# Row maxima turned in a bank of their own, and the first expert tile's up products moved ahead of the last attention outputs

## The chip, the cores and the metric

The kernel runs on one core of a Trainium2 chip. The metric is the device time of one execution in microseconds (us): three runs of the kernel before gave 564.69, 566.49 and 567.13 us, median 566.49 us. The engines are named as the profile names them: PE (TensorE, matrix products), PEld (its weight loads), DVE (VectorE), ACT (ScalarE), POOL (GpSimd) and SP (SyncE, which here only issues transfers). They run side by side, each through its own list of instructions in order, and wait for one another at counters (semaphores).

## The reference

Sixteen sequences of 256 tokens of width 128 go through a mixture-of-experts layer, causal attention with 16 heads of width 8, and the same mixture-of-experts layer again:

```python
x = L0_attn_x                                   # (16, 256, 128)
x = x + 0.5 * _L0_ffn_ref(_layernorm(x), gate_w, w1, w2, w3)   # 8 experts, the best 2 of each token
x = x + _L0_attn_ref(_layernorm(x), WQ, WK, WV, WO)
x = x + 0.5 * _L0_ffn_ref(_layernorm(x), gate_w, w1, w2, w3)

# attention: score = QK^T / sqrt(8) + causal mask; score -= rowmax(score); softmax; times V; times WO
# experts:   y = (silu(x w1) * (x w3)) w2 for each expert, weighted by the two gates
```

## The kernel before

The program has three stages. In the first (to about 183 us of the profiled execution) the tokens are routed and go through the experts in tiles of 256 rows, called units; the second (about 183 to 409 us) is attention; the third is the second expert layer, again in units. One unit is `tile_up`, 12 matmuls into the banks `B_H1` and `B_H3`, then a SiLU on ACT, a product on DVE, and `tile_down`. A tile's rows come from memory through a transposing load that SP issues (`load`, L476); SP issues the first load of the third stage only when the last scores are done and every scattered row of that set has landed (L526).

Attention runs as 16 steps, `step(b, ...)` with b from 0 to 15, one for each sequence. A step has eight rounds (u on PE, k on DVE), one for each pair of heads. In a round PE makes a pair's scores for a sequence that is up to two steps ahead (`score_products`, L1753, with `score_masks`, L1770); DVE takes their row maxima (`row_max`, L1322), and there is a single buffer for these scores, so that the next pair's scores wait for this reduction. PE also makes the transposed scores of sequence b itself (`score_t_products`, L1783, and L1790 and L1792 for the mask), ACT takes their exponentials (L953), and PE multiplies these by the values (`values`, L1816 and L1819).

Two chains run beside this and share PSUM bank 7, `B_M1`, whose uses are counted by `m1_ready` (written) and `m1_freed` (read):

- The row maxima of sequence b+1: in round 3 DVE combines them (`combine_max`, L1330 to L1332), POOL clamps them (`clamp`, L698), in round 4 PE turns them (`max_transpose`, L1801 to L1803), ACT copies them out (L941), and SP places them for the next step's products.
- The outputs of sequence b-1: in rounds 1 and 3 PE turns their halves back (`o_back`, L1831), each is normalised by DVE (`o_norm`, L1339 and L1341), in round 5 PE turns both (`o_transpose`, L1838), ACT and DVE copy them out as a high and a low half (L945, L1347), in round 7 PE multiplies by WO (`o_project`), and DVE adds to x (`x_add`, L1351).

So bank 7 has five uses in a step: half 0, half 1, the maxima, the transposed outputs, the projection. A use waits until the use before has been freed, and `max_transpose` waits for two things, the clamp and the second `o_norm`:

```python
            def max_transpose(b, q, use):
                pe.wait_ge(clamp_done, done(b))
                if not isinstance(use, int) or use > 0:
                    pe.wait_ge(m1_freed, use)
```

In the steps without a previous sequence or without a next one, `no_use` counts an empty use on DVE, ACT and PE.

Behind step 15 the last outputs are finished between the first units of the third stage. PE's order there is written out by hand: `values(15, 3, 3)`, both `o_back`, `tile_up(2, 0)`, `o_transpose`, `tile_up(2, 1)`, `o_project`, `tile_up(2, 2)`, and then `tile_down` and `tile_up` in turn. DVE's order beside it is `highest` (gates of a routed set), `o_norm` of half 0, `second` (more gates, L1142 to L1149), `o_norm` of half 1, `product` of unit 0. The units' banks 0 to 3 are the banks of the scores and transposed scores; bank 4, free in attention, takes every second `tile_down` of the units.

Of the kernel before, what the change touches and what calls it, by code (L numbers as in the profile page):

```python
# [38 lines left out]
SEQ = 256  # L39
# [7 lines left out]
PAIRS = 8  # L47
# [58 lines left out]
def build_macaron(nc, x_in, w_up1, w_up3, w_down, w_small, out, batches):  # L106
# [8 lines left out]
    with ctx:  # L115
# [188 lines left out]
        m1_ready = sem("m1_ready")  # L304
        m1_freed = sem("m1_freed")
# [128 lines left out]
        def m1_use(b):  # L434
            return 5 * b - 1

        def max_use(b):

            return m1_use(b) + 2
# [3 lines left out]
        def max_bank(use):  # L443

            return B_M1 if use else B_EARLY
# [3 lines left out]
        def _(sp):  # L449
# [311 lines left out]
        def _(act):  # L761
# [174 lines left out]
            def max_copy(b, q, use):  # L936

                act.wait_ge(m1_ready, done(use))
                if not isinstance(b, int) or b > 1:
                    act.wait_ge(m_placed, 32 * (b - 1))  # L940
                s_.activation(negmax_t[0:HEADS, q % 2, :], bank[0:HEADS, max_bank(use), 0:SEQ], ACT.Copy).then_inc(m1_freed, 1)  # L941
# [5 lines left out]
            def step(b, q, G, prev=True, route=None):  # L947
                for u in range(PAIRS):
# [17 lines left out]
                    if u == 4:  # L966
                        if b_ok(b + 1):
                            max_copy(b + 1, q + 1, max_use(b))
                        else:
                            no_use(act, max_use(b), m1_freed)  # L970
                        if route is not None:
                            rows_high(1, route)
                    if u == 5:
                        if prev:
                            o_high(m1_use(b) + 3)
                        o_copy(b, q, 0)
# [5 lines left out]
            def first_groups(n):  # L982
                g, which = first_step(n)
                if which == 0:
                    x_high(m0_use(g), g)
                if which == 1:
                    q_high(g, g)
                if which == 2:
                    k_high(g, g)
                if which == 3:  # L990
                    act.wait_ge(vaug_set, 2)
                    v_copy(g, g)
                if n == MAX_TURN + 1:
                    max_copy(0, 0, 0)
# [47 lines left out]
        def _(dve):  # L1042
# [306 lines left out]
            def x_add(b, u0, tail=False):  # L1349
                dve.wait_ge(m1_ready, done(u0 + (3 if tail else 4)))  # L1350
                v_.scalar_tensor_tensor(x_tile(tile_of(b - 1), 2), bank[:, B_M1, 0:2 * D], 1.0 / WSCALE,  # L1351
                                        x_tile(tile_of(b - 1), 2), ALU.mult, ALU.add).then_inc(m1_freed, 1)

            def step(b, q, G, prev=True, adds=(), route=None, buf=None):
                odd = q % 2 == 1
                for k in range(PAIRS):
# [18 lines left out]
                    if not prev and k == 7:  # L1375
                        no_use(dve, max_use(b) + 1, m1_freed)
                        no_use(dve, max_use(b) + 2, m1_freed)
                    if k in (5, 7) and adds:
                        add(*adds[k // 7])
                    if route is not None:  # L1380
                        if k == 0:

                            dve.wait_ge(m1_freed, m1_use(b - 1) + 5)
                            statistics(1, route, buf)
# [87 lines left out]
            x_add(batches, M1_TAIL, tail=True)  # L1472
# [34 lines left out]
        def _(pe):  # L1507
# [288 lines left out]
            def max_transpose(b, q, use):  # L1796
                pe.wait_ge(clamp_done, done(b))
                if not isinstance(use, int) or use > 0:
                    pe.wait_ge(m1_freed, use)
                dst = bank[0:HEADS, max_bank(use), 0:SEQ]  # L1800
# [3 lines left out]
                    .then_inc(m1_ready, 1)  # L1804
# [20 lines left out]
            def o_back(b, q, u0, qb):  # L1825
# [3 lines left out]
                pe.wait_ge(m1_freed, use)  # L1829
# [18 lines left out]
            def step(b, q, G, prev=True, route=None):  # L1848
                par = (q // 2 + 1) % 2
                for u in range(PAIRS):  # L1850
# [16 lines left out]
                    if u == 4:  # L1867
                        if b_ok(b + 1):
                            max_transpose(b + 1, q + 1, max_use(b))
                        else:  # L1870
# [10 lines left out]
                    if u == 7:  # L1881
                        if route is not None:
                            gate(route)
                        if prev:
                            o_project(m1_use(b) + 4)
                        else:
                            for use in (max_use(b) + 1, max_use(b) + 2):
                                pe.wait_ge(m1_freed, use)
                                no_use(pe, use, m1_ready)
# [7 lines left out]
            def first_groups(n):  # L1897
# [13 lines left out]
                if n == MAX_TURN:  # L1911
                    pe.wait_ge(s_reduced, done(PAIRS + AHEAD - 1, D_S))
                    max_transpose(0, 0, 0)
# [63 lines left out]
```

## Time and profile before

| | |
|---|---|
| median of 3 runs | 566.49 us (564.69 to 567.13) |
| the profiled execution's own time | 565.05 us |
| its span in the trace | 563.0 us |
| PE busy | 501.2 us, 89% of the span |
| DVE, ACT, POOL busy | 373.7, 317.2, 267.9 us |
| granted TensorE clock, mean | 0.993 of full speed |

The span is the stretch that the trace covers; 2.05 us of the execution's time lie outside it. A time given as "at 409.6" is counted from the start of the span. The busy shares are means over stages that have different limits, so what an edit is worth is read in its own stage.

### The profile page before, as it was taken

The numbers are of one execution on the slowest core, as the hardware profiler recorded it, in microseconds if no ns is written. First come the engines' busy times: TensorE is split into PE (matmuls) and PEld (weight loads), VectorE is DVE, ScalarE is ACT, GpSimd is POOL, SyncE is SP. The second block draws the span as 40 slices with busy tenths as digits, with TensorE's granted clock in tenths as the row PEclk, the third lists the DMA queues.
The fourth block names the chain that finished last, engine by engine and source line by source line (L and its number), as shares of the span: only waits on it lengthen the run. The fifth ranks groups of instructions, "written<-read, shape, count | busy, mean of one in ns | idle before, by whom it ended". The sixth has DMA issues, their size and how long they took to land.

```text
span 563.0 us, 19023 instructions
## 1 busy us (share of the span) xinstructions
PE 501.2 (89%) x7286; PEld 411.0 (73%) x7286; DVE 373.7 (66%) x995; ACT 317.2 (56%) x597; POOL 267.9 (48%) x325
## 2 busy tenths in 40 slices
PE   1689999999999788898889886888889999999995
PEld 1679998988889456565656554655579999999995
DVE  5656865324675789999898898776375532455665
ACT  4945654433335576767676765667744444445553
POOL 7967877612463323333431111565607601666662
PEclk9999999999999799999999999999999999999999
DMA  9971247786764314846212120311147755843222
GB/s 271 306 242 50 61 100 161 175 157 155 129 138 121 102 59 108 245 109 186 79 58 62 41 60 2 119 57 36 45 94 164 155 133 130 156 119 91 72 75 56
DMA packets 114661, 65.86 MB, mean 117 GB/s; under 512 B 51856, under 2 KB 108432, under 8 KB 114576
## 3 DMA queue, kind: packets, MB, share of 16 engines
q1 hardware_dynamic: 84400, 38.95, 27.0%
q0 software_dynamic: 6912, 14.17, 10.0%
q10 hardware_dynamic: 23264, 11.54, 8.3%
q8 instruction: 61, 1.00, 0.8%
q14 instruction: 24, 0.20, 0.1%
HBM read 18.88 MB, written 34.87 MB: 95 GB/s over the span
## 4 chain that ended last, share of the span: by engine, by line
PE 61%; DVE 20%; ACT 6%; DMA 5%; issue 4%; POOL 1%; SPq 1%; ACTq 0%; DVEq 0%; POOLq 0%
PE bank L1641 19%; PE bank L1522 10%; PE bank L1524 10%; PE bank L1523 10%; DVE negmax L1322 8%; ACT pt L953 3%; PE bank L1753 3%; PE bank L1534 2%; PE bank L1816 2%; PE bank L1783 2%; DMA yg<-sorted_y,row 2%; DVE X L1219 2%; PE bank L1831 1%; ACT r_xn L785 1%; ACT ot L933 1%
## 5 line engine op out<-in xcount | busy, mean ns | idle before, releaser
L689 POOL DMA_INDIRECT yg<-sorted_y,row x108 | 104.1, 964 | 141.7 <-PE bank L1641 45.7
L1210 DVE SCALAR_TENSOR_TENSOR pt<-bank,pt 128x512 f32<-128x512 f32 x122 | 84.3, 691 | 118.3 <-PE bank L1524 109.8
L953 ACT ACTIVATE pt<-bank 128x768 f32<-128x768 f32 x128 | 104.1, 813 | 72.2 <-PE bank L1792 71.7
L675 POOL DMA_INDIRECT sorted_x<-xs,row x108 | 106.5, 987 | 52.0 <-issue 22.5
L1641 PE MATMUL bank<-w,pt 128*128 (+1 forms) x976 | 130.0, 277 | 0.0
L1641 PEld LDWEIGHTS bank<-w,pt 128*128 128x128 f32 x976 | 118.6, 192 | 3.2
L1322 DVE TENSOR_REDUCE negmax<-bank 128x10 f32<-128x640 f32 x128 | 104.4, 816 | 17.1 <-PE bank L1770 15.3
L829 ACT ACTIVATE pt<-bank 128x512 f32<-128x512 f32 x122 | 72.8, 597 | 26.3 <-PE bank L1524 25.1
L837 ACT ACTIVATE yb<-bank 128x256 f32<-128x256 f32 x82 | 31.5, 384 | 79.5 <-PE bank L1641 72.9
L1753 PE MATMUL bank<-zc 63*64 63x64 f16 (+3 forms) x1024 | 43.0, 244 | 16.6 <-DVE negmax L1322 13.8
L1753 PEld LDWEIGHTS bank<-zc 63*64 63x64 f16 x1024 | 18.9, 105 | 43.6 <-DVE negmax L1322 29.3
L1783 PE MATMUL bank<-zc 64*64 64x256 f16 (+1 forms) x1024 | 44.1, 248 | 3.5 <-ACT pt L953 3.2
L1816 PE MATMUL bank<-pt,vaug 128*32 128x256 f32 x512 | 41.5, 394 | 5.1 <-ACT ot L933 4.8
L1522 PE MATMUL bank<-pt,w1h 128*128 128x256 f16 x164 | 45.0, 274 | 1.0 <-DMA pt<-sorted_x 0.7
L1523 PE MATMUL bank<-pt,w3h 128*128 128x256 f16 x164 | 45.0, 275 | 0.0
L1524 PE MATMUL bank<-pt,w1l 128*128 128x256 f16 x164 | 45.0, 275 | 0.0
L1522 PE MATMUL bank<-pt,w3h 128*128 128x256 f16 x164 | 45.0, 275 | 0.0
L1523 PE MATMUL bank<-pt,w1h 128*128 128x256 f16 x164 | 45.0, 274 | 0.0
L1524 PE MATMUL bank<-pt,w3l 128*128 128x256 f16 x164 | 45.0, 274 | 0.0
L858 ACT ACTIVATE ot<-bank,comb 128x128 f32<-128x128 f32 x80 | 25.1, 364 | 35.1 <-PE bank L1641 35.1
L1219 DVE SCALAR_TENSOR_TENSOR X<-yg,weight,X 128x128 f32<-128x128 f32 x108 | 37.7, 349 | 3.4 <-DMA yg<-sorted_y,row 1.4
L1792 PE MATMUL bank<-causal_t,ident_b 64*64 64x256 bf16 x256 | 35.8, 273 | 0.0
(171 smaller groups left out, 1015.8 us busy)
## 6 DMA issues: line engine op xcount, KB each, us to landing
sorted_y<-yb ACTq DMA_DIRECT2D x82, 128.0 KB
sorted_x<-zeros SPq DMA_DIRECT2D x2, 2944.0 KB, 14.5
zc<-qk_rows SPq DMA_DIRECT2D x84, 64.0 KB
qk_rows<-qksplit SPq DMA_DIRECT2D x8, 512.0 KB, 2.8
sorted_x<-zeros SPq DMA_DIRECT2D x1, 2432.0 KB, 11.4
sorted_x<-zeros SPq DMA_DIRECT2D x1, 2176.0 KB, 10.3
X<-x_in SPq DMA_DIRECT2D x8, 256.0 KB, 5.1
zc<-w_up SPq DMA_DIRECT2D x8, 256.0 KB, 6.7
```

Of the source, the lines that this page charges most:

```text
L675: ps.indirect_dma_start(out=sorted_x[s], out_offset=bass.IndirectOffsetOnAxis(ap=row[:, s, k, t:t + 1], axis=0), in_=xs[:, R0[s] + t, :], ...
L689: ps.indirect_dma_start(out=yg[:, a % D_YG, k, :], out_offset=None, in_=sorted_y[s], in_offset=bass.IndirectOffsetOnAxis(ap=row[:, s, k, t ...
L829: s_.activation(silu[:, n % D_H], bank[:, B_H1 + n % 2, :], ACT.Silu, scale=1.0 / WSCALE)\
L953: s_.activation(pt[:, hg, (u % 2) * 768:(u % 2 + 1) * 768].rearrange("p (a n) -> p a n", a=2), bank[:, B_ST:B_ST + 2, 0:384], ACT.Exp, sca ...
L1210: v_.scalar_tensor_tensor(hid[:, n % D_HID], bank[:, B_H3 + n % 2, :], 1.0 / WSCALE, silu[:, n % D_H], ALU.mult, ALU.mult).then_inc(prod_d ...
L1322: v_.tensor_reduce(negmax[:, q % 2, k, :, 0:PARTS], bank[:, b0:b0 + 2, 0:S_COLS].rearrange("p a (s k) -> p a s k", k=HALF), AX.X, ALU.max, ...
L1522: t_.matmul(dst, ah, bh, start=True, stop=False)
L1523: t_.matmul(dst, ah, bl, start=False, stop=False)
L1524: return t_.matmul(dst, al, bh, start=False, stop=True)
L1641: last = t_.matmul(y_half(n)[:, u * D:(u + 1) * D], hid[:, n % D_HID, c * SLOTS + u * P:c * SLOTS + (u + 1) * P], w2[:, bass.ds(offset + c ...
L1753: t_.matmul(bank[side(g), b0 + a, c0:c0 + keys], zc[rows, par, 0, u, q0:q0 + HALF], zc[rows, par, 1, u, e * SEQ:e * SEQ + keys], start=n = ...
L1783: t_.matmul(bank[side(g), B_ST + a, kb * SEQ:SEQ + kb * P], zc[side(a), par, 1, u, k0 + HALF * g:k0 + HALF * (g + 1)], zc[side(a), par, 0, ...
```

## The change

The turned maxima move from bank 7 to bank 4 and get counters of their own, `max_ready` and `max_freed`; bank 7 keeps four uses in a step, and `no_use` goes. In the hand-written order behind step 15, `tile_up(2, 0)` and its wait move ahead of both `o_back`. DVE's, ACT's, POOL's and SP's own orders stay as they were.

```diff
-        def no_use(eng, use, count):
-            if count is m1_freed:
-                eng.wait_ge(m1_freed, use)
-                eng.wait_ge(m1_ready, use + 1)
-            eng.sem_inc(count, 1)
...
         def m1_use(b):
-            return 5 * b - 1
-        def max_use(b):
-            return m1_use(b) + 2
+            return 4 * b - 4
...
-        def max_bank(use):
-            return B_M1 if use else B_EARLY
+        B_MAX = 4
+
+        def max_bank(b):
+            return B_MAX if b else B_EARLY
...
-                hold(sp, m1_freed, (max_use(b - 1) + 1) if not isinstance(b, int) or b > 0 else 1)
+                hold(sp, max_freed, b + 1)
...
-            def max_copy(b, q, use):
-                act.wait_ge(m1_ready, done(use))
+            def max_copy(b, q):
+                act.wait_ge(max_ready, b + 1)
...
-            def max_transpose(b, q, use):
+            def max_transpose(b, q):
                 pe.wait_ge(clamp_done, done(b))
-                if not isinstance(use, int) or use > 0:
-                    pe.wait_ge(m1_freed, use)
-                dst = bank[0:HEADS, max_bank(use), 0:SEQ]
+                if b > 1:
+                    pe.wait_ge(max_freed, b)
+                dst = bank[0:HEADS, max_bank(b), 0:SEQ]
...
-                            max_transpose(b + 1, q + 1, max_use(b))
-                        else:
-                            pe.wait_ge(m1_freed, max_use(b))
-                            no_use(pe, max_use(b), m1_ready)
+                            max_transpose(b + 1, q + 1)
                     if u == 5 and prev:
-                        o_transpose(m1_use(b) + 3)
+                        o_transpose(m1_use(b) + 2)
...
             values(batches - 1, 3, 3)
+            pe.wait_ge(exp_done, done(PAIRS * batches - 1, D_ST))
+            tile_up(2, 0)
             o_back(batches, 0, M1_TAIL, 0)
             o_back(batches, 0, M1_TAIL, 1)
-            pe.wait_ge(exp_done, done(PAIRS * batches - 1, D_ST))
-            tile_up(2, 0)
             o_transpose(M1_TAIL + 2)
             tile_up(2, 1)
```

The order of PE's instructions in round 4 of step 2, of the kernel before: the last masks of the transposed scores, the three products that turn the maxima, and the first of `values`.

```order
L1790 MATMUL bank<-causal_t,ident_b 64x2x64
L1792 MATMUL bank<-causal_t,ident_b 64x2x128
L1801 MATMUL bank<-ident_h,negmax_h 16x128 [waits m1_freed,clamp_done]
L1802 MATMUL bank<-ident_h,negmax_h 16x64
L1803 MATMUL bank<-ident_h,negmax_h 16x64
L1816 MATMUL bank<-pt,vaug 32x256 [waits exp_done]
```

And of the changed kernel, whose line numbers are 11 lower here:

```order
L1779 MATMUL bank<-causal_t,ident_b 64x2x64
L1781 MATMUL bank<-causal_t,ident_b 64x2x128
L1790 MATMUL bank<-ident_h,negmax_h 16x128 [waits max_freed,clamp_done]
L1791 MATMUL bank<-ident_h,negmax_h 16x64
L1792 MATMUL bank<-ident_h,negmax_h 16x64
L1805 MATMUL bank<-pt,vaug 32x256 [waits exp_done]
```

No instruction moved; the first product waits for `max_freed` in place of `m1_freed`, and for the clamp as before.

PE's order behind step 15, of the kernel before: the end of `values`, both `o_back` (L1831), and the first products of `tile_up(2, 0)`, which start with a wait for the first load (`xt_loaded6`).

```order
L1819 MATMUL bank<-pt,vaug 32x128 x4
L1831 MATMUL bank<-ident,ot 128x128 [waits m1_freed,o_copied]
L1831 MATMUL bank<-ident,ot 128x128 x3
L1831 MATMUL bank<-ident,ot 128x128 [waits m1_freed,o_copied]
L1831 MATMUL bank<-ident,ot 128x128 x3
L1522 ISA [waits silu_done,xt_loaded6,exp_done]
L1522 MATMUL bank<-qksplit,w1h 128x256
L1523 MATMUL bank<-qksplit,w1h 128x256
```

The changed kernel at the same place:

```order
L1808 MATMUL bank<-pt,vaug 32x128 x4
L1511 ISA [waits silu_done,xt_loaded6,exp_done]
L1511 MATMUL bank<-qksplit,w1h 128x256
L1512 MATMUL bank<-qksplit,w1h 128x256
```

The wait for the load now stands ahead of both `o_back`.

Further on in the changed kernel, from the last products of `tile_up(2, 0)` to the wait at the head of `tile_up(2, 1)`:

```order
L1513 REGISTER_ALU
L1513 MATMUL bank<-qksplit,w3l 128x256
L1821 MATMUL bank<-ident,ot 128x128 [waits m1_freed,o_copied]
L1821 MATMUL bank<-ident,ot 128x128 x3
L1821 MATMUL bank<-ident,ot 128x128 [waits m1_freed,o_copied]
L1821 MATMUL bank<-ident,ot 128x128 x3
L1828 MATMUL bank<-ident,on 128x128 [waits m1_freed]
L1828 MATMUL bank<-ident,on 128x128
L1511 ISA [waits silu_done,xt_loaded7]
```

Both `o_back` (L1821) and `o_transpose` (L1828) now follow one another with no unit's products between them.

## Rows read from the trace of the kernel before

**Rows 1.** The page's head, busy times and chain that ended last, whole execution.

```profile
span 563.0 us, 19023 instructions
PE 501.2 (89%) x7286; PEld 411.0 (73%) x7286; DVE 373.7 (66%) x995; ACT 317.2 (56%) x597; POOL 267.9 (48%) x325
...
PE 61%; DVE 20%; ACT 6%; DMA 5%; issue 4%; POOL 1%; SPq 1%; ACTq 0%; DVEq 0%; POOLq 0%
```

**Rows 2.** Busy time by stretch: attention, then experts; length first, then each engine.

```profile
183.00:403.00 220.00, 186.25 (x4385) 124.39 (x4387) 185.83 (x501) 144.20 (x225) 82.22 (x102) 0.98 0.30 86
...
420.00:553.00 133.00, 133.00 (x1214) 124.82 (x1214) 69.34 (x162) 65.30 (x145) 68.98 (x72) 1.00 0.52 120
```

**Rows 3.** Who waited for whom, 180 to 440: total us, times, longest.

```profile
PE bank L1753 <- DVE negmax L1322: 13.8, 33, 1.4
...
PE bank L1801 <- DVE on L1341: 5.4, 13, 0.6
```

**Rows 4.** Timeline of step 4, round 4: start, duration, instruction, idle before and releaser.

```profile
247.81 0.29 DVE L1341 TENSOR_TENSOR on<-bank,rden 128x128 f32<-128x128 f32 x1
...
247.63 0.35 POOL L698 TENSOR_SCALAR negmax_h<-negmax 128x32 f16<-128x32 f32 x1 [1.25 <-DVE negmax L1332]
...
248.24 0.22 PE L1801 MATMUL bank<-ident_h,negmax_h 128*16 128x128 f16 x1 [0.17 <-DVE on L1341]
...
249.10 0.33 PE L1753 MATMUL bank<-zc 63*64 63x64 f16 x8
```

**Rows 5.** The same of step 3, round 4.

```profile
233.89 0.29 DVE L1341 TENSOR_TENSOR on<-bank,rden 128x128 f32<-128x128 f32 x1
...
233.76 0.35 POOL L698 TENSOR_SCALAR negmax_h<-negmax 128x32 f16<-128x32 f32 x1 [2.54 <-DVE negmax L1332]
...
234.32 0.22 PE L1801 MATMUL bank<-ident_h,negmax_h 128*16 128x128 f16 x1 [0.64 <-DVE on L1341]
...
235.51 0.33 PE L1753 MATMUL bank<-zc 63*64 63x64 f16 x8 [0.26 <-DVE negmax L1322]
```

**Rows 6.** PE's timeline behind step 15.

```profile
409.19 0.40 PE L1819 MATMUL bank<-pt,vaug 128*32 128x128 f32 x8
410.31 0.66 PE L1831 MATMUL bank<-ident,ot 128*128 128x128 f32 x4 [0.72 <-ACT ot L933]
411.80 0.63 PE L1831 MATMUL bank<-ident,ot 128*128 128x128 f32 x4 [0.84 <-DVE on L1341]
412.26 0.27 PE L1522 MATMUL bank<-qksplit,w1h 128*128 128x256 f16 x1
...
414.08 0.44 PE L1838 MATMUL bank<-ident,on 128*128 128x128 f32 x2 [0.34 <-DVE on L1341]
414.35 0.27 PE L1522 MATMUL bank<-qksplit,w1h 128*128 128x256 f16 x1
...
415.66 0.22 PE L1522 MATMUL bank<-wsh,oh 128*128 128x128 f16 x1
```

**Rows 7.** DVE's timeline beside it.

```profile
411.07 0.26 DVE L1339 RECIPROCAL rden<-bank 128x16 f32<-128x16 f32 x1 [0.56 <-PE bank L1831]
411.37 0.29 DVE L1341 TENSOR_TENSOR on<-bank,rden 128x128 f32<-128x128 f32 x1
...
413.73 0.29 DVE L1341 TENSOR_TENSOR on<-bank,rden 128x128 f32<-128x128 f32 x1
413.94 0.68 DVE L1210 SCALAR_TENSOR_TENSOR pt<-bank,pt 128x512 f32<-128x512 f32 x1
```

**Rows 8.** SP's first loads of the third stage, L476, 408 to 426.

```profile
L476 SPq DMA_TRANSPOSE qksplit<-sorted_x x12: 1215/1264/1981, 408.5 to 424.5; - x12
...
DMA to landing us min/median/max: 2.7/2.7/4.6
```

**Rows 9.** Around step 0: busy time, granted clock third from the end; PE's timeline.

```profile
186.00:192.80 6.80, 6.13 (x96) 3.81 (x100) 4.37 (x16) 2.85 (x5) 3.33 (x5) 0.50 0.43 112
192.80:196.00 3.20, 2.07 (x68) 1.36 (x60) 2.79 (x8) 2.71 (x5) 2.22 (x3) 1.00 0.11 28
...
183.77 0.33 PE L1753 MATMUL bank<-zc 63*64 63x64 f16 x8 [0.53 <-issue]
...
185.08 0.33 PE L1753 MATMUL bank<-zc 63*64 63x64 f16 x8 [0.65 <-DVE negmax L1322]
...
186.34 0.54 PE L1783 MATMUL bank<-zc 64*64 64x256 f16 x8 [0.87 <-ACT pt L953]
```

More of the change, by code:

```diff
@@ L304, in build_macaron @@
         m1_ready = sem("m1_ready")
+        max_ready = sem("max_ready")
+        max_freed = sem("max_freed")
         m1_freed = sem("m1_freed")
@@ L934, in o_copy @@
                              bank[:, B_O, :], ACT.Copy).then_inc(o_copied, 1)
-            def max_copy(b, q, use):
-                act.wait_ge(m1_ready, done(use))
+            def max_copy(b, q):
+                act.wait_ge(max_ready, b + 1)
                 if not isinstance(b, int) or b > 1:
                     act.wait_ge(m_placed, 32 * (b - 1))
-                s_.activation(negmax_t[0:HEADS, q % 2, :], bank[0:HEADS, max_bank(use), 0:SEQ], ACT.Copy).then_inc(m1_freed, 1)
+                s_.activation(negmax_t[0:HEADS, q % 2, :], bank[0:HEADS, max_bank(b), 0:SEQ], ACT.Copy)\
+                    .then_inc(max_freed, 1)
             def o_high(use):
@@ L974, in step @@
                         if prev:
-                            o_high(m1_use(b) + 3)
+                            o_high(m1_use(b) + 2)
                         o_copy(b, q, 0)
@@ L993, in first_groups @@
                 if n == MAX_TURN + 1:
-                    max_copy(0, 0, 0)
+                    max_copy(0, 0)
             def first_stack(n):
@@ L1347, in o_low, with x_add @@
                 v_.tensor_tensor(ol[:, :], bank[:, B_M1, 0:SEQ], oh[:, :], ALU.subtract).then_inc(m1_freed, 1)
-            def x_add(b, u0, tail=False):
-                dve.wait_ge(m1_ready, done(u0 + (3 if tail else 4)))
+            def x_add(b, u0):
+                dve.wait_ge(m1_ready, done(u0 + 3))
                 v_.scalar_tensor_tensor(x_tile(tile_of(b - 1), 2), bank[:, B_M1, 0:2 * D], 1.0 / WSCALE,
@@ L1374, in step @@
                         add(0, EARLY + k // 2)
-                    if not prev and k == 7:
-                        no_use(dve, max_use(b) + 1, m1_freed)
-                        no_use(dve, max_use(b) + 2, m1_freed)
                     if k in (5, 7) and adds:
@@ L1381, in step @@
                         if k == 0:
-                            dve.wait_ge(m1_freed, m1_use(b - 1) + 5)
+                            dve.wait_ge(m1_freed, m1_use(b - 1) + 4)
                             statistics(1, route, buf)
@@ L1471, in _ @@
             product(U_SECOND + 1)
-            x_add(batches, M1_TAIL, tail=True)
+            x_add(batches, M1_TAIL)
             product(U_SECOND + 2)
@@ L1803, in max_transpose @@
                 t_.matmul(dst[:, P + HALF:SEQ], negmax_h[:, q % 2, 1, :], ident_h[:, 0:HALF], start=True, stop=True)\
-                    .then_inc(m1_ready, 1)
+                    .then_inc(max_ready, 1)
             def values(b, q, hg):
@@ L1828, in o_back @@
                 pe.wait_ge(o_copied, done(2 * (b - 1) + 1, D_O))
-                pe.wait_ge(m1_freed, use)
+                if use > 0:
+                    pe.wait_ge(m1_freed, use)
                 for hg in range(HG):
@@ L1884, in step @@
                         if prev:
[L1885 to L1889, printed above, removed]
+                            o_project(m1_use(b) + 3)
                     if b == ROUTED + 2:
@@ L1912, in first_groups @@
                     pe.wait_ge(s_reduced, done(PAIRS + AHEAD - 1, D_S))
-                    max_transpose(0, 0, 0)
+                    max_transpose(0, 0)
             def first_set(slot):
```

4 lines of the change are left out of this document (1 added, 3 removed).

## The prediction

> **What bounds the kernel now.** I read the page's head first: PE is busy for 501.2 of 563.0 us and carries 61% of the chain that ended last [rows 1]. Then the stretches. From 420 to 553 PE is busy for all of the 133.00 us, at full clock: the second expert layer is PE's own work without a gap, so whatever delays PE's entry into it comes out in the end time one for one, and nothing behind gives it back. In attention neither engine is full: from 183 to 403 PE is busy for 186.25 and DVE for 185.83 of 220 us [rows 2]. They take turns, since PE's next scores wait for DVE's reduction of the last (33 waits, 13.8 us in all) [rows 3]. So a gap on PE that closes in attention counts only where PE, and not DVE, ends last in the round behind it.
>
> The list of waits then shows what the first part of the change touches: PE sat idle 5.4 us in 13 waits before L1801, the turning of the maxima, put down to L1341, the second normalisation [rows 3]. The timeline of PE, DVE and SP behind step 15 is the last view, because the second part reorders PE there.
>
> **Part 1: the maxima leave bank 7.** The removed wait is the one for L1341. What remains is the clamp on POOL. In step 4 the clamp ends at 247.63 + 0.35 = 247.98 and the normalisation at 247.81 + 0.29 = 248.10; PE starts the turning at 248.24, 0.14 after the later of them [rows 4]. In step 3 the clamp ends at 234.11, the normalisation at 234.18, and PE starts at 234.32 [rows 5]. So the wait that takes the place of the removed one ends 0.12 and 0.07 us earlier, not 0.4. These two steps are one of each kind, odd and even, and both engines run the same two lists of instructions in all 14 steps that have the turning and a previous sequence, so I take 0.1 us a step and not more.
>
> Does the 0.1 reach the end? In step 4 PE goes from the turning through the value products into the next scores at 249.10 without a wait, so PE is last there and 0.1 us is won [rows 4]. In step 3 the next scores start at 235.51 after 0.26 us of idling for DVE's reduction, which doesn't depend on the turning; there nothing is won [rows 5]. With half of the 14 steps like step 4 that is 7 x 0.1 = 0.7 us at most; some of it is lost again at later waits for DVE, and I take 0.5. The bounds are 0 (every such 0.1 us ends in a wait for DVE) and 14 x 0.12 = 1.7 us (none does).
>
> Other edits of this part cost nothing. The turned outputs in round 5 waited for ACT's copy of the maxima and now wait for the second normalisation, an earlier event, and PE has no idle row there. The copy, the placing and their transfers follow the turning by the same instructions. The empty uses of steps 0 and 15 carried no work. Bank 4 is not written by a unit in attention.
>
> The Trainium skill speaks for this part (Perfetto Trace Analysis, Optimizing Tensor Performance, Matmuls): independent groups of matmuls should rotate through different PSUM banks, so that one bank's evacuation overlaps the next group's products. By that rule the whole listed wait would go. The trace doesn't agree, as the two clamp rows show: with the bank free, the data is not there yet.
>
> **Part 2: `tile_up(2, 0)` ahead of both `o_back`.** Before, PE ends `values` at 409.59, waits 0.72 us for ACT's copy, runs the first `o_back` from 410.31, waits 0.84 us for the first normalisation, runs the second from 411.80 and goes straight into `tile_up(2, 0)` at 412.26. That fills the time in which DVE works through `second`: the second normalisation ends only at 413.73 + 0.29 = 414.02, `o_transpose` starts at 414.08 after 0.34 us, and PE is dense from there [rows 6, 7].
>
> The idea to fill the 0.72 us with unit 0 meets the load. SP issues the first one at 408.5, and such loads land 2.7 us after issue in the median here, also at the least [rows 8]: 408.47 + 2.7 = 411.2. PE runs its list in order, so both `o_back` now stand behind a wait that ends at 411.2 instead of 410.3. Step by step:
>
> - `tile_up(2, 0)` starts at 411.2. Its 12 matmuls take as long as those of `tile_up(2, 1)`, from 414.35 to the next product at 415.66: 1.31 us [rows 6]. So the first `o_back` starts at 412.5.
> - From the start of the first `o_back` to DVE's reciprocal are 411.07 - 410.31 = 0.76 us, and from there to the end of the second normalisation 414.02 - 411.07 = 2.95, since `second` stands between the two on DVE [rows 6, 7]. That gives 412.5 + 0.76 + 2.95 = 416.2. The second `o_back` (at 411.80 - 411.07 = 0.73 behind the reciprocal, so 414.0) is long done.
> - `o_transpose` starts 0.06 later, at 416.3, against 414.08: 2.2 us later. In between PE idles from about 414.6 to 416.3, where `tile_up(2, 0)` used to be.
>
> Behind `o_transpose` both orders are equal, the product of unit 0 (413.94 before) moves with the second normalisation and is still in time for unit 2, and PE is the bound. So the handover costs 2.2 us. Its bounds: if the load had landed before 409.6, PE would go into it at once, the first `o_back` would start at 410.9 in place of 410.31, and the cost would be 0.6; if it landed 4.6 us after issue, the longest such time [rows 8], 1.9 us more, 4.1. I stay with 2.2, as the two loads in flight are those of before and nothing new runs beside them.
>
> **Sum.** Against the profiled execution, 565.05 us (563.0 of span and 2.05 around it): -0.5 + 2.2 = +1.7, so 566.8. That execution was 1.4 us under the median of the runs; on the median the forecast is 566.5 + 1.7 = 568.2 us, 0.3% more. What a measurement of this kernel can tell from no change is about 0.5%, or 2.8 us.
>
> **The rivals.**
> *The clock falls in the handover (slower).* Around step 0 PE idled 0.53, 0.65 and 0.87 us between short bursts, 2.05 us out of some 3.1, and from 186.0 to 192.8 the granted clock was 0.50, 1.2 GHz [rows 9]. In my schedule PE idles 0.8 and 1.7 us between 413.2 and 416.3, 2.5 out of 3.1; so the stretch is at least as empty, while the one of before, with 0.72, 0.84 and 0.34 [rows 6], kept 2.4 GHz. What follows is dense work on the bound engine, where a stretch at half clock loses half of itself: 3.4 us for one as long as 6.8, 1.7 for one half as long. That gives 569.9 to 571.6 us. Against it: the expert products between the gaps are denser than what ran in step 0. [...] Chance 0.28. The Trainium skill (Perfetto Trace Analysis, Matmul Optimizations) says that this engine scales with its utilization, so that matmuls should run back to back in batches; the rows of step 0 agree.
> *The bank was the wait (faster).* All 5.4 us before L1801 vanish: 566.5 + 2.2 - 5.4 = 563.3. For it speaks the list of waits, against it the end of the clamp in both steps. Chance 0.04.
> *The load is hidden (no change).* If it lands about 1 us sooner than the median says, the handover costs 0.6 and the steps give 0.5: 566.6. Nothing in the rows has one landing under 2.7. Chance 0.10.
> *The load is late.* 4.6 us: 568.2 + 1.9 = 570.1. Chance 0.05.
>
> **How the numbers follow.** My forecast has 0.50; 0.03 is left for what I don't see. The time is that of the forecast, 568.2. The range runs from 566.3, just under the hidden load (566.6) and the forecast with the full 1.7 us from the steps (567.0), to 571.0, inside the clock's case, whose shorter stretch is the likelier one. Faster by over 0.5% (under 563.7): 0.04. Slower by over 0.5% (over 569.3): the clock's case but for a little, part of the late load, and the forecast's upper edge, 0.29. Within: 0.67.
>
> **What would show each step.** In the changed profile the wait before the turning (now L1790) is put down to POOL's clamp, with 4 to 5 us in 13 or 14 waits; if it is under 2 us, the bank was the wait. Attention, from its first scores to the end of the last `values`, is 0 to 1.7 us shorter. Behind step 15 PE waits for the load, for some 1.6 us from the end of `values`, the first products of unit 0 come 0.9 us after the place where the first `o_back` stood, `o_transpose` waits some 1.7 us for L1341's successor, and comes 6.7 us behind the end of `values` where it was 4.5. The granted clock of the following 7 us is 1.00, or 0.50 in part if the rival holds. The prediction is wrong if PE doesn't wait for the load, if the second expert layer has gaps that take the delay in, or if the steps change by more than 2 us either way.

## The result and the profile after

The changed kernel takes 569.42 us (median of 6 runs, 568.0 to 570.29). The kernel before, run beside it on the same chip, takes 565.62 us (6 runs, 562.46 to 567.13). The ratio is 1.0074, with a 95% interval of 1.0047 to 1.0101: the change makes the kernel 3.8 us slower, where 1.7 were forecast. (A ratio here and below is worked out from the runs and is not the quotient of the two medians, which is 1.0067; a difference in us is one of medians.) The profiled execution took 569.17 us against 565.05, 4.1 more, so its trace holds the whole loss.

The page's head of the changed kernel, to be laid beside [rows 1], and its two stretches beside [rows 2]:

```profile
span 567.1 us, 19015 instructions
PE 505.5 (89%) x7286; PEld 412.6 (73%) x7286; DVE 373.8 (66%) x995; ACT 316.3 (56%) x597; POOL 267.9 (47%) x325
```

```profile
183.00:403.00 220.00, 188.88 (x4404) 125.40 (x4406) 186.11 (x501) 144.24 (x226) 82.26 (x102) 0.99 0.31 89
420.00:553.00 133.00, 133.00 (x1225) 124.91 (x1223) 69.80 (x168) 64.77 (x144) 66.69 (x71) 1.00 0.51 119
```

The second expert layer is as full as before, 133.00 of 133.00 us at full clock, so nothing behind the handover gave anything back. The loss lies ahead of that stretch. PE's timeline behind step 15, beside [rows 6], shows where:

```profile
409.20 0.40 PE L1808 MATMUL bank<-pt,vaug 128*32 128x128 f32 x8
411.56 0.28 PE L1511 MATMUL bank<-qksplit,w1h 128*128 128x256 f16 x1 [1.96 <-issue]
...
412.88 0.60 PE L1821 MATMUL bank<-ident,ot 128*128 128x128 f32 x4
414.31 0.63 PE L1821 MATMUL bank<-ident,ot 128*128 128x128 f32 x4 [0.83 <-DVE on L1333]
416.58 0.69 PE L1828 MATMUL bank<-ident,on 128*128 128x128 f32 x2 [1.64 <-DVE on L1333]
417.06 0.42 PE L1511 MATMUL bank<-qksplit,w1h 128*128 128x256 f16 x1
```

PE ends `values` at 409.60, the same time as before, waits 1.96 us for the first load, and makes `tile_up(2, 0)` and both `o_back`; `o_transpose` starts at 416.58 against 414.08. The profile puts the 1.96 us down to "issue"; that it is the wait for the load follows from the order of the instructions and from the load's issue at 408.66, 2.9 us before these products. In the seven traces in which PE waits at this place, the products start 2.8 to 3.0 us behind the issue. The last two rows show a second thing: `o_transpose` takes 0.69 us where it took 0.44, and a product of a unit 0.42 where it took 0.27. PE works slower there. The windows behind it say the same, with the granted clock third from the end (0.51, the 1.2 GHz level, then 0.99, the 2.4 GHz level):

```profile
416.40:419.80 3.40, 3.22 (x16) 2.41 (x17) 1.15 (x3) 0.98 (x2) 0.00 (x0) 0.51 0.36 82
419.80:424.00 4.20, 4.20 (x51) 3.92 (x49) 2.99 (x12) 1.68 (x4) 0.30 (x2) 0.99 0.29 62
```

DVE's timeline beside it answers to [rows 7]. The second normalisation (L1333) stands behind the gates, as it did, and so follows the first by 2.4 us wherever that starts:

```profile
413.58 0.26 DVE L1331 RECIPROCAL rden<-bank 128x16 f32<-128x16 f32 x1 [3.07 <-PE bank L1821]
413.88 0.29 DVE L1333 TENSOR_TENSOR on<-bank,rden 128x128 f32<-128x128 f32 x1
...
416.24 0.29 DVE L1333 TENSOR_TENSOR on<-bank,rden 128x128 f32<-128x128 f32 x1
```

The last long block of products of PE's stage closes the account. It is L1641 before and L1630 after; the first row is of before, the second of after:

```profile
554.11 2.94 PE L1641 MATMUL bank<-w,pt 128*128 128x128 f32 x24
```

```profile
558.19 2.93 PE L1630 MATMUL bank<-w,pt 128*128 128x128 f32 x24
```

From the end of `values` to this block are 554.11 - 409.59 = 144.5 us before and 558.19 - 409.60 = 148.6 after, 4.1 more. Of these, 2.5 lie ahead of `o_transpose` (6.98 us behind the end of `values`, against 4.49), and 1.6 behind it (141.61 to the block, against 140.03). The second part fits the stretch at half clock: 3.4 us long, and half of it lost.

In attention the first part of the change can be read off the waits and the timeline. The list of waits before the turning, beside [rows 3], 195 to 403 us:

```profile
PE bank L1742 <- DVE negmax L1314: 13.8, 30, 1.4
...
PE bank L1790 <- POOL negmax_h L691: 5.3, 9, 1.8
```

Then the two steps of [rows 4] and [rows 5], step 4 first, then step 3, and the turning and the next scores of step 5, since the row of those scores is missing in step 3. The third fence is step 5 of the kernel before:

```profile
249.10 0.35 POOL L691 TENSOR_SCALAR negmax_h<-negmax 128x32 f16<-128x32 f32 x1 [1.25 <-DVE negmax L1324]
249.28 0.29 DVE L1333 TENSOR_TENSOR on<-bank,rden 128x128 f32<-128x128 f32 x1
249.51 0.22 PE L1790 MATMUL bank<-ident_h,negmax_h 128*16 128x128 f16 x1
```

```profile
234.18 0.35 POOL L691 TENSOR_SCALAR negmax_h<-negmax 128x32 f16<-128x32 f32 x1 [2.52 <-DVE negmax L1324]
234.59 0.22 PE L1790 MATMUL bank<-ident_h,negmax_h 128*16 128x128 f16 x1 [0.48 <-POOL negmax_h L691]
...
263.35 0.22 PE L1790 MATMUL bank<-ident_h,negmax_h 128*16 128x128 f16 x1 [0.48 <-POOL negmax_h L691]
264.70 0.33 PE L1742 MATMUL bank<-zc 63*64 63x64 f16 x8 [0.41 <-DVE negmax L1314]
```

```profile
262.03 0.22 PE L1801 MATMUL bank<-ident_h,negmax_h 128*16 128x128 f16 x1 [0.41 <-DVE on L1341]
...
263.22 0.33 PE L1753 MATMUL bank<-zc 63*64 63x64 f16 x8 [0.27 <-DVE negmax L1322]
```

The bank is free, and the clamp sets the start. In step 4 it ends at 249.45, PE starts at 249.51, before the normalisation is over (249.57), and no idle time is left where 0.17 us stood. In step 3 the idle time falls from 0.64 to 0.48. In step 5 the next scores wait 0.41 for DVE where they waited 0.27: what the turning won, the next wait takes.

### The profile page after: what moved, and what is told of

Same layout as the page of the kernel before. It is cut to its first block, busy times and chain, and to the rows that moved or that the text cites. A ratio compares the mean times of both kernels' runs of the same rounds, so it can differ in the third digit from the quotient of the medians.

```text
span 567.1 us, 19015 instructions
## 1 busy us (share of the span) xinstructions
PE 505.5 (89%) x7286; PEld 412.6 (73%) x7286; DVE 373.8 (66%) x995; ACT 316.3 (56%) x597; POOL 267.9 (47%) x325
## 4 chain that ended last, share of the span: by engine, by line
PE 62%; DVE 21%; ACT 5%; issue 5%; DMA 4%; POOL 1%; SPq 1%; ACTq 0%; DVEq 0%; POOLq 0%
PE bank L1630 18%; PE bank L1511 10%; PE bank L1513 10%; PE bank L1512 10%; DVE negmax L1314 8%; PE bank L1742 3%; ACT pt L947 2%; PE bank L1523 2%; PE bank L1805 2%; DVE X L1211 2%; PE bank L1772 1%; PE bank L1821 1%; ACT r_xn L778 1%; DVE xn L1058 1%; DVE rden L1331 1%
## 5 line engine op out<-in xcount | busy, mean ns | idle before, releaser
L1630 PE MATMUL bank<-w,pt 128*128 (+1 forms) x976 | 130.0, 277 | 0.0
L1630 PEld LDWEIGHTS bank<-w,pt 128*128 128x128 f32 x976 | 118.6, 192 | 3.1
```

Source lines behind the costliest of these rows:

```text
L1630: last = t_.matmul(y_half(n)[:, u * D:(u + 1) * D], hid[:, n % D_HID, c * SLOTS + u * P:c * SLOTS + (u + 1) * P], w2[:, bass.ds(offset + c ...
```

## The experiments

Each kernel is compared with the kernel before, run in turn with it on the same chip. The first batch and the third met the same conditions (kernel before at 564.59 and 563.98 us); the second ran on another chip, on which the kernel before takes 608.36 us, so its numbers are compared within the batch alone. Each trace is of one execution. Line numbers are those of the changed kernel, but for `order_only`, which has those of before, and `clamp_twice`, whose turning is L1794 and clamp L695.

Two theories stood at the start. **The handover and the clock:** the first expert unit ahead of `o_back` puts a wait for the load, 2.5 us, on PE's path, and the gaps it makes bring the clock down for 1.6 more; the bank costs nothing. **The bank:** the turning, at another time or in another bank, costs something in attention, and part of the loss is there.

### Each part alone

`bank_only` has bank 4 and its counts, with the order behind step 15 as before:

```diff
             values(batches - 1, 3, 3)
-            pe.wait_ge(exp_done, done(PAIRS * batches - 1, D_ST))
-            tile_up(2, 0)
             o_back(batches, 0, M1_TAIL, 0)
             o_back(batches, 0, M1_TAIL, 1)
+            pe.wait_ge(exp_done, done(PAIRS * batches - 1, D_ST))
+            tile_up(2, 0)
             o_transpose(M1_TAIL + 2)
```

> The maxima in bank 4 with their own counts, as in the changed kernel; the order behind step 15 as before. Theory A (the handover and the clock behind it cost, the bank gains a little): 564.6 us against 565.6 before, 0 to 1.7 us faster; the turning starts 0.05 us behind the clamp in place of 0.21 to 0.26, the attention steps from the first turning to the end of the last values are about 1 us shorter, and from there to the transposed outputs it takes 4.5 us as before, at full clock. Theory B (the steps themselves got slower, by a new wait for POOL or a changed balance of PE and DVE, and the handover is only part of it): 566.5 us or more.

Measured: 564.86 us, ratio 1.0008 (0.9981 to 1.0035). `order_only` is the reverse, the kernel before with `tile_up(2, 0)` and its wait ahead of both `o_back`, bank 7 shared as before:

> The up products of the first unit ahead of both turned outputs, the maxima in bank 7 as before. Theory A: the handover is 2.5 us longer (7.0 in place of 4.5 from the end of the last values to the transposed outputs) and the clock falls behind it in most executions, 1.6 us more; 569.5 us, 3 to 4.5 us over before. Theory B: at most 2.5 us over before, 568.1, the rest of the measured loss being the bank's.

Measured: 569.53 us, ratio 1.0079 (1.0050 to 1.0108). The loss is all in the order. The 11 runs lie between 566.4 and 572.4 us, and the only trace is of one at 569.85; whether the clock fell in the quicker ones too is not shown. The trace of `order_only` repeats the handover, gap by gap, and the half clock behind it:

```profile
412.19 0.28 PE L1522 MATMUL bank<-qksplit,w1h 128*128 128x256 f16 x1 [1.80 <-issue]
413.51 0.60 PE L1831 MATMUL bank<-ident,ot 128*128 128x128 f32 x4
414.94 0.63 PE L1831 MATMUL bank<-ident,ot 128*128 128x128 f32 x4 [0.84 <-DVE on L1341]
417.21 0.44 PE L1838 MATMUL bank<-ident,on 128*128 128x128 f32 x2 [1.64 <-DVE on L1341]
```

```profile
417.90:421.20 3.30, 3.30 (x21) 2.51 (x20) 1.49 (x3) 0.77 (x2) 0.00 (x0) 0.50 0.21 48
```

`bank_only` at the same place, behind an `o_transpose` that starts 4.56 us behind the end of `values`, stays at the 2.4 GHz level, and reaches the last block in 144.6 us, as the kernel before:

```profile
412.00:416.00 4.00, 3.76 (x37) 3.50 (x38) 2.53 (x6) 1.58 (x3) 0.00 (x0) 1.00 0.45 103
```

### The gaps filled

`filled` is the changed kernel with products that nobody reads (identity by a tile of `xh`, into bank 4) in the two long gaps. They move no wait. If only the late `o_transpose` costs, the time is that of the change; if the gaps bring the clock down, 1.6 us come back.

```diff
+            def filler(n):
+                for k in range(n):
+                    t_.matmul(bank[:, 4, 0:SEQ], ident_h[:, :], xh[:, 0, 0:SEQ], start=True, stop=True,
+                              skip_group_check=True)
             values(batches - 1, 3, 3)
+            filler(16)
             pe.wait_ge(exp_done, done(PAIRS * batches - 1, D_ST))
             tile_up(2, 0)
             o_back(batches, 0, M1_TAIL, 0)
             o_back(batches, 0, M1_TAIL, 1)
+            filler(14)
             o_transpose(M1_TAIL + 2)
```

> The changed kernel with 16 spare matmuls of 256 columns ahead of the wait for the first load and 14 ahead of the transposed outputs, into bank 4, which nobody reads before it is written anew; they run only where PE idled. If the clock is a part of the loss: granted clock 1.00 behind step 15, 567.3 us, about 1.6 us under the changed kernel, with the transposed outputs still 7.0 us behind the last values. If the gaps cost only their own length: 569.4 as the changed kernel.

Measured: 566.77 us, ratio 1.0039 (1.0018 to 1.0061). Its timeline has both fillers, and `o_transpose` where it was in the changed kernel, 6.89 us behind the end of `values`:

```profile
409.74 1.92 PE L1912 MATMUL bank<-xh,ident_h 128*128 128x256 f16 x16
411.67 0.28 PE L1511 MATMUL bank<-qksplit,w1h 128*128 128x256 f16 x1
...
414.89 1.69 PE L1912 MATMUL bank<-xh,ident_h 128*128 128x256 f16 x14
416.70 0.44 PE L1828 MATMUL bank<-ident,on 128*128 128x128 f32 x2
```

```profile
416.40:419.80 3.40, 3.28 (x33) 2.85 (x32) 2.29 (x5) 1.30 (x3) 0.00 (x0) 1.00 0.36 83
```

The window that stood at 0.51 is at 1.00. The first unit's products start 2.8 us behind the load's issue at 408.86, so the first filler doesn't hold them up. From `o_transpose` to the last block are 556.73 - 416.70 = 140.03 us, the number of the kernel before to the hundredth. So 1.6 us of the loss are the clock's, and the gaps are its cause. The medians agree: 2.2 us over the kernel before beside it, where the changed kernel was 3.8 over. Which of the two gaps it takes is not separated, since `filled` fills both. The Trainium skill (Perfetto Trace Analysis, Matmul Optimizations) says that the matmul engine scales its power with its use and wants products back to back in batches; the two windows agree, 0.51 with the gaps and 1.00 with them filled.

### The second normalisation earlier

`norm_first` is the changed kernel with the second `o_norm` ahead of the gates on DVE, to take the 1.6 us gap away and leave the wait for the load.

```diff
             o_norm(batches, M1_TAIL, 0)
-            second(R0[3], RT[3], 3)
             o_norm(batches, M1_TAIL, 1)
+            second(R0[3], RT[3], 3)
```

> The changed kernel with the second normalisation of the last outputs ahead of the second half of the gates on DVE. If the transposed outputs are late because DVE does the gates between the two normalisations: they come 6.1 us behind the last values in place of 7.0, and the product of unit 0 about 1.4 us later, which unit 2 just meets; with the gap shortened to 0.7 us the clock holds in most executions; 567.2 us. If the load alone sets the handover: 569.4, no change.

Measured: 569.41 us, ratio 1.0073 (1.0049 to 1.0098), a miss. In its trace (567.02 us, one of the quick runs) the gap is 0.68 us, `o_transpose` starts 6.06 us behind the end of `values`, and the clock holds, as expected. But a new wait stands behind it, the third row:

```profile
413.50 0.63 PE L1821 MATMUL bank<-ident,ot 128*128 128x128 f32 x4 [0.84 <-DVE on L1333]
414.80 0.44 PE L1828 MATMUL bank<-ident,on 128*128 128x128 f32 x2 [0.68 <-DVE on L1333]
...
417.62 0.23 PE L1511 MATMUL bank<-wsh,oh 128*128 128x128 f16 x1 [1.06 <-DVE ol L1339]
```

`o_project` waits for DVE's low half, ahead of which the gates and the first unit's product now stand: the delay moved by one wait. The 12 runs lie apart, 5 at 565.85 to 567.58 and 7 at 569.37 to 571.30, and the only trace is of the first five. Whether the clock fell in the seven is not shown: the granted clock is on record only as each run's mean, 0.988 to 0.998 in the five and 0.983 to 0.991 in the seven, which leans that way and doesn't say where it fell. This kernel tells of the moved wait and of nothing else.

### On the second chip

`after_again` is the changed kernel once more.

> The changed kernel once more, beside the next three on one chip, and a second trace of it. 569 us, 3.8 us over before; the transposed outputs 7.0 us behind the last values, and 142.96 us from them to PE's last product if the clock holds there, 144.5 if it falls for 3.4 us. Theory A (order and clock) expects the fall in most executions, so here too.

Measured: 610.92 us, ratio 1.0030 (0.9999 to 1.0061), a smaller loss. In its trace the first load is issued 2.0 us before the end of `values` (in the changed kernel's first trace 0.9), PE waits for it 0.85 us, and `o_transpose` comes 5.9 us behind the end. The half clock is there all the same:

```profile
443.24 0.40 PE L1808 MATMUL bank<-pt,vaug 128*32 128x128 f32 x8
444.49 0.28 PE L1511 MATMUL bank<-qksplit,w1h 128*128 128x256 f16 x1 [0.85 <-issue]
...
449.52 0.44 PE L1828 MATMUL bank<-ident,on 128*128 128x128 f32 x2 [1.65 <-DVE on L1333]
```

```profile
450.20:453.50 3.30, 3.30 (x21) 2.50 (x20) 1.49 (x3) 0.78 (x2) 0.00 (x0) 0.50 0.22 48
```

PE's wait is 1.1 us shorter and `o_transpose` comes 1.1 us sooner than in the first trace, so the handover costs less where the load is issued earlier. That this makes the whole smaller loss is argued: no trace of the kernel before was taken on this chip, and the interval reaches from no loss into that of the first measurement.

`spread` keeps bank 4 and puts each piece where its data is ready: half 0 before the load, unit 0 while DVE normalises, half 1, unit 1 in the time of the gates, then `o_transpose`.

```diff
             values(batches - 1, 3, 3)
+            o_back(batches, 0, M1_TAIL, 0)
             pe.wait_ge(exp_done, done(PAIRS * batches - 1, D_ST))
             tile_up(2, 0)
-            o_back(batches, 0, M1_TAIL, 0)
             o_back(batches, 0, M1_TAIL, 1)
-            o_transpose(M1_TAIL + 2)
             tile_up(2, 1)
-            o_project(M1_TAIL + 3)
+            o_transpose(M1_TAIL + 2)
             tile_up(2, 2)
+            o_project(M1_TAIL + 3)
```

> The maxima in bank 4, and behind step 15 another order: first turned half, up products of unit 0, second turned half, up products of unit 1, transposed outputs, up products of unit 2, projection. If the loss comes from a load's wait ahead of the first turned half and from an empty PE beside DVE's gates, this order has neither: PE idles about 1 us in place of 1.9 behind step 15, clock 1.00, 0.9 us under the kernel with the bank alone and 1 to 2 us under before: 563.2. If any up products ahead of the outputs cost: 565 or more.

Measured: 606.43 us, ratio 0.9968 (0.9937 to 0.9999). In its trace PE has no wait between the first `o_back` and `o_transpose`, and the clock stays at 1.00. `turn_late` has bank 4 and the old order behind step 15, and in round 4 of a step the turning goes behind the value products:

```diff
-                    if u == 4:
-                        if b_ok(b + 1):
-                            max_transpose(b + 1, q + 1)
...
                     if u in (2, 4, 6):
                         values(b, q, u // 2 - 1)
+                    if u == 4:
+                        if b_ok(b + 1):
+                            max_transpose(b + 1, q + 1)
```

> The maxima in bank 4, the order behind step 15 as before, and in each step the turning behind round 4's value products, so that these fill PE's wait for the clamp (0.36 to 0.49 us in every second step). If such a wait pays only where PE ends last: the wait goes, PE's idling before the next scores grows from 0.4 to 0.8 us, and the time stays within 1 us of the kernel with the bank alone, 564.9. If every wait of PE in a step pays: 4 us less, 561.

Measured: 606.47 us, ratio 0.9955 (0.9925 to 0.9986). The wait before the turning is gone, and the next scores wait 0.95 us, where they wait 0.42 in the same step of `spread`:

```profile
283.10 0.22 PE L1790 MATMUL bank<-ident_h,negmax_h 128*16 128x128 f16 x1
284.33 0.33 PE L1742 MATMUL bank<-zc 63*64 63x64 f16 x8 [0.95 <-DVE negmax L1314]
```

`clamp_twice` has bank 4 and the old order too, and POOL does the clamp twice, one behind the other, to see what a later clamp costs.

```diff
                 ps.tensor_scalar(negmax_h[:, q % 2], part[:, 0:PARTS + 1:PARTS, :],
+                                 -MLIMIT, MLIMIT, ALU.max, ALU.min).then_inc(first_clamp, 1)
+                pool.wait_ge(first_clamp, b + 1)
+                ps.tensor_scalar(negmax_h[:, q % 2], part[:, 0:PARTS + 1:PARTS, :],
                                  -MLIMIT, MLIMIT, ALU.max, ALU.min).then_inc(clamp_done, 1)
```

> The maxima in bank 4, the order behind step 15 as before, and POOL clamps twice, 0.4 us more each step. If the clamp is what the turning waits for: it starts 0.4 us later against DVE's second normalisation in all 14 steps, which costs the 7 steps where PE ends last 0.4 us each, 2.8 us: 567.5. If the clamp is covered: 564.9, no change.

Measured: 621.10 us, ratio 1.0218 (1.0162 to 1.0274): 12.7 us, far more than the 2.8 expected. The wait before the turning grew as it should, from 4.5 us (the row of `spread`) to 11.9, and another wait grew beside it: DVE's sums of the first expert layer, which run in attention's first steps, wait for rows that POOL's queue gathers behind the second clamp. `clamp_twice` first, then `spread`, waits of PE and of DVE:

```profile
PE bank L1794 <- POOL negmax_h L695: 11.9, 15, 1.1
...
DVE X L1215 <- DMA yg<-sorted_y,row: 4.8, 2, 2.7
```

```profile
PE bank L1790 <- POOL negmax_h L691: 4.5, 10, 0.5
...
DVE X L1211 <- DMA yg<-sorted_y,row: 0.8, 1, 0.8
```

These two account for 7.4 and 4.0 us of waiting, 11.4 together. That is a sum of waits and not of time lost, and two more things differ between the traces: PE waits 25.7 us for DVE's row maxima where it waits 21.2 in `spread` (160 to 460 us), and the granted clock in attention is 0.95 in the mean where it is 0.97. So the run shows that a later clamp costs, and how the 12.7 us are made up stays open.

### The third batch

These runs repeat the two questions that were left, whether the bank gains anything and whether the better order does. `bank_again` is `bank_only`, `spread_again` is `spread`, `both` has the order of `spread` and the late turning, and `after_third` is the changed kernel.

> The kernel with the bank alone once more, beside the next three on one chip. If the bank's gain is the 0.5 to 1.2 us that the traces of attention show, 0.1 to 0.2% under before, inside what can be told from no change. If it is more than that (the turning late of the last batch was 0.45% under before, and holds the bank's part): 0.3% or more.

> The kernel with the bank and the units' up products between the last outputs. Theory A: the handover idles PE about 1 us less than before's, and with the bank's gain 1.5 to 2 us, 0.3%, under before, as in the last batch (0.32%), and about 1 us under the bank alone. If the last batch's difference was scatter: equal to before.

> The bank, the turning behind round 4's value products, and the up products between the last outputs. If the two edits add: 0.13% more than the turning late (0.45%), about 3 us under before. If the turning late won nothing of its own: as the kernel without it, 0.3%.

> The changed kernel. If the first load's landing sets the handover, its loss goes with PE's wait for that load in the trace: 3.8 us where the wait is 2 us, as in the first trace, and 1.8 us where it is 0.85 us, as in the second; the clock's part, up to 1.7 us, comes on top where the granted clock is 0.50 behind the transposed outputs.

| kernel | median, us | ratio to before | 95% interval |
|---|---|---|---|
| `bank_again` | 565.33 | 1.0021 | 0.9995 to 1.0047 |
| `spread_again` | 563.80 | 0.9987 | 0.9963 to 1.0011 |
| `both` | 563.60 | 0.9973 | 0.9949 to 0.9996 |
| `after_third` | 569.39 | 1.0103 | 1.0061 to 1.0144 |

The timeline of `spread_again` shows why its order works. PE waits 0.78 us for ACT's copy and 0.41 for the load, and no more up to `o_transpose`, which finds its data ready:

```profile
410.04 0.66 PE L1821 MATMUL bank<-ident,ot 128*128 128x128 f32 x4 [0.78 <-ACT ot L926]
411.10 0.28 PE L1511 MATMUL bank<-qksplit,w1h 128*128 128x256 f16 x1 [0.41 <-issue]
412.42 0.60 PE L1821 MATMUL bank<-ident,ot 128*128 128x128 f32 x4
414.17 0.38 PE L1828 MATMUL bank<-ident,on 128*128 128x128 f32 x2
```

```profile
552.89 2.93 PE L1630 MATMUL bank<-w,pt 128*128 128x128 f32 x24
```

From the end of `values` (409.25) to the last block are 143.6 us, 0.9 less than before and 5.0 less than in the changed kernel; the medians of the batch lie 5.6 us apart. Neither kernel is clearly quicker than before: `both` has the lowest median of the batch, 0.27% under the kernel before by the ratio and 0.07% by the medians, and `spread_again` has an interval that holds 1. `turn_late` had the lowest ratio of the study, 0.9955, but `both`, which adds it to `spread`, took 563.60 us beside the 563.80 of `spread_again`, so the late turning shows no gain of its own. All of these lie within the 0.5% that the prediction took as telling. `after_third` waits 2.02 us for the load and has the half clock in the same place (0.50 from 417.6 to 421.0). It lost 5.4 us, more than the 3.8 of the first measurement, with 148.7 us from the end of `values` to the last block where the first trace had 148.6; what makes up the rest is not shown.

## Why the prediction was right and where it was wrong

The measured 569.42 us lie between the stated 566.3 and 571.0, and the loss of 0.74% is on the side that had a chance of 0.29. The forecast itself, 568.2, was too small: the range held the result because it had been drawn into the case of the rival that then came true.

**What bounds the kernel: right.** The second expert layer had no gap to take the delay in; the 4.1 us of the trace arise between 409.6 and 419.8 and arrive at the end whole.

**The handover, +2.2: right in each step, 0.3 short.** PE waits for the load, then `o_back`, the gates and the second normalisation follow at their old distances. The load was issued at 408.66, 0.19 later than before, and its products start at 411.56, 2.9 behind, where the text took 2.7 for the landing and nothing between landing and start. These two are the 0.3 and a little more. Measured: 6.98 - 4.49 = 2.5 us. The forecast said 1.6 us of waiting for the load, 1.7 for `o_transpose` and 6.7 from `values` to it; the trace has 1.96, 1.64 and 6.98.

**The clock: the step that failed.** The prediction weighed "PE idles 0.8 and 1.7 us" against the denser expert products between them, gave the falling clock 0.28, and took as likeliest that it holds. It falls, in all four traces that have this order with the gaps open (the changed kernel three times, `order_only` once), beginning between 0.2 us ahead of the start of `o_transpose` and 0.7 behind it, for 3.4 us each time, and at this place in none of the others: not in `bank_only` or `bank_again`, `spread`, `spread_again` or `both`, `turn_late` or `clamp_twice`, nor in `norm_first`, whose second gap is 0.68 instead of 1.64, nor in `filled`. `filled` makes it a shown cause. Its price is the smaller of the two named, 1.6 us where 1.7 stood. The rival's sum, +3.4 to +5.1 us, holds the measured +3.8, and the forecast is less than half of it; the times that the rival named, 569.9 to 571.6, begin above the measured 569.42, since the kernel before took 565.62 beside it and not 566.49. The miss was one of weighing: the rows of step 0 showed a clock that had fallen on gaps no larger in sum, and a dense spell of 1.3 us between the gaps was taken for a reason against, on no row.

**The steps, -0.5: the mechanism right, the counting wrong, the gain not seen in the whole time.** The list of waits has the turning behind the clamp, as said, but 5.3 us in 9 waits, where 4 to 5 in 13 or 14 were forecast. 1.8 of the 5.3 are a single wait in step 0, where the clock had not fallen in this run; `bank_only` has 3.5 us in 8. The prediction took seven of the 14 steps to be like step 4. In the trace of the kernel before only five are, steps 1, 2, 4, 6 and 8, with 0.17 or 0.18 us of idle time each; eight wait 0.41 to 0.64 us, and step 12 has none. In those five no wait is left. The 0.1 us a step came out as 0.17, because PE starts 0.05 us behind the clamp now and 0.14 behind the later of two before.

Five steps of 0.17 are 0.9 us. From the turning of step 1 to the end of `values` two traces with bank 7 have 202.6 us (before) and 201.9 (`order_only`), and the six with bank 4, the old turning and full clock there have 200.4 to 201.9, mean 201.4. So the means lie 0.9 us apart, and single traces overlap. What PE no longer waits before the turning it waits in part before the next scores: from 206 to 409 us its waits for DVE's row maxima are 12.0 and 12.1 us in the two traces with bank 7, and 12.9 to 13.4 in the six with bank 4. The medians show no gain: `bank_only` stands at +0.08% and `bank_again` at +0.21%, where 0.9 us would be -0.16%, inside the first interval (down to -0.19%) and below the second (down to -0.05%). What else takes the gain back, if anything does, stays open.

**The other rivals.** That the bank was the wait is out: the turning still waits for the clamp. The rule of the Trainium skill weighed there (Perfetto Trace Analysis, Optimizing Tensor Performance) would have taken the whole listed wait away; in the trace it fell by 0.17 us in step 4 and by 0.16 in step 3. The hidden load is out on this chip (PE waited 1.96 us), and comes near on the second, where PE waited 0.85 us and the loss was 0.30%. The late load did not come: the first ten loads of the third stage in the changed kernel landed within 2.7 us.

**The parts add up.** Handover +2.5, clock +1.6, steps between -0.9 (traces) and about +0.8 (mean of the two ratios of the bank alone): +3.2 to +4.9, measured +3.8.

## What to carry to other kernels

- Work put into an idle gap brings its own wait along. An engine that runs a list in order pays for the latest of what stands ahead; so an item goes where its data is ready, not merely where the engine is free. Here the same pieces cost 3.8 us in one order and nothing in another.
- When a reordering opens gaps ahead of dense products, price the clock with the gaps. If a trace shows anywhere that the clock fell on gaps of such a size, take it as the likelier case, and test it with products that nobody reads.
- A list of waits names only the releaser that came last. What a wait costs once that one is gone is read from the end of the other one, and whether it counts is read at the next wait behind it.

## What the runs showed of the hardware

- Products that nobody reads kept the clock at 2.4 GHz: 16 and 14 of them, 1.9 and 1.7 us of PE's time, in place of idle gaps of 1.96 and 1.64 us, brought the granted clock from 0.51 to 1.00 and the loss against the kernel before from 3.8 us to 2.2.
- The turning, with only POOL's clamp to wait for, started 0.05 us behind the clamp's end, and `o_transpose`, with only DVE to wait for, 0.06 behind the normalisation (414.02 to 414.08 before). With both engines to wait for, in the kernel before, the turning was 0.14 behind the later one.
- Single profiles of one program differ by where the clock falls. The first trace of the changed kernel has no half clock around attention's step 0 (second row) and 3.4 us of it in the middle of attention (first row); `after_third`, the same program, has 3.4 us at step 0 (third row), and the kernel before 6.8 [rows 9]:

```profile
341.40:344.80 3.40, 3.40 (x67) 2.07 (x64) 3.00 (x14) 1.41 (x2) 0.48 (x2) 0.50 0.02 5
...
186.00:192.80 6.80, 4.69 (x136) 3.01 (x131) 5.90 (x18) 4.47 (x6) 1.31 (x2) 1.00 0.47 119
```

```profile
188.90:192.30 3.40, 3.08 (x52) 1.48 (x49) 2.58 (x9) 1.62 (x2) 0.35 (x1) 0.50 0.37 99
```

  The seven traces on the first chip with bank 4 and the turning in its old place end `values` between 407.7 and 409.9 us, so a difference of 1 us between two whole stages says nothing, and stages are compared from an instruction inside them.
- Another chip took 608.36 us for the kernel before, 8% more, and the same change cost 0.30% there. Why that chip is slower no run shows; its load was issued 2.0 us before the end of `values` where it was 0.9 on the first.
